# A transformer kernel with V and q products issued inside the feed-forward block, feed-forward weights split at the layer border, and the global norm's inverse on ScalarE

## The reference, cut to what matters

```
x = attn_layer(shift_tokens(x), Wqkv[i], q_scale[i], k_scale[i], Wo[i]) + x
x = ffn_layer(shift_tokens(x), ln_g[i], ln_b[i], W1[i], b1[i], W2[i], b2[i]) + x
```

## Time and profile before

| | |
|---|---|
| median of 3 runs | 3241.17 us (3239.01 to 3252.73) |
| profiled execution, its own time | 3247.59 us |
| its span, first to last instruction | 3245.8 us |
| busy share PE / DVE / ACT / POOL | 97% / 84% / 78% / 75% |
| mean granted TensorE clock | 0.988 of 2.4 GHz |

### The profile page before, as it was taken

The page is one execution under the profiler, slowest core; times in us unless marked ns, Lnnn a source line. Parts: engine busy times, 40 slices in busy tenths (PEclk is TensorE's granted clock), DMA queues, the critical chain, the costliest instruction groups (busy, mean ns, idle before and its releaser), DMA issues. The chain is left out here.

```text
span 3245.8 us, 151130 instructions
## 1 busy us (share of the span) xinstructions
PE 3132.2 (97%) x63141; PEld 2614.1 (81%) x63141; DVE 2712.8 (84%) x6367; ACT 2522.3 (78%) x5220; POOL 2442.1 (75%) x1536
## 2 busy tenths in 40 slices
PE   7869999999999999999999999999999999999996
PEld 6757888888888888888888888888888888888885
DVE  6559888888888888888888888888888888888883
ACT  3337888887888888888888888888888888788884
POOL 6458787787777777777777778777777777777773
PEclk9889999999999999999999999999999999999998
DMA  4551111132111122211122211122111122121111
GB/s 168 195 189 47 45 44 46 46 88 72 50 43 45 50 81 63 63 42 47 50 81 63 63 45 44 47 79 70 57 50 44 45 79 72 56 57 45 47 54 29
DMA packets 109237, 211.00 MB, mean 65 GB/s; under 512 B 19344, under 2 KB 40080, under 8 KB 104592
## 3 DMA queue, kind: packets, MB, share of 16 engines
q1 hardware_dynamic: 106544, 193.36, 20.2%
q10 hardware_dynamic: 2016, 7.98, 0.7%
HBM read 46.91 MB, written 28.53 MB: 23 GB/s over the span
## 5 line engine op out<-in xcount | busy, mean ns | idle before, releaser
L456 POOL TENSOR_TENSOR qks<-work 128x1024 f32<-128x1024 f32 x384 | 910.2, 2370 | 524.9 <-DVE work L1216 508.1
L843 PE MATMUL psum<-wparts,xhi 128*128 128x512 f32 x2304 | 788.6, 423 | 14.9 <-POOL xlo L442 8.0
L464 POOL TENSOR_TENSOR qkr<-qks,rnorm 128x1024 f32<-128x1024 f32 x384 | 731.5, 1905 | 0.4
L605 ACT ACTIVATE sq<-psum 128x512 f32<-128x512 f32 x768 | 455.3, 593 | 117.8 <-PE psum L843 90.0
L1214 DVE TENSOR_TENSOR work<-psum,rot 128x512 f32<-128x512 f32 x768 | 523.6, 682 | 6.1 <-ACT sq L605 3.7
L1187 DVE TENSOR_REDUCE ssq<-sq 128x8 f32<-128x512 f32 x768 | 475.9, 657 | 0.0
L843 PE MATMUL psum<-wparts,xlo 128*128 128x512 f32 x1152 | 454.5, 395 | 0.0
L927 PEld LDWEIGHTS psum<-probT,vsh 64*64 64x64 f32 x12288 | 326.2, 134 | 140.6 <-issue 140.2
L843 PEld LDWEIGHTS psum<-wparts,xhi 128*128 128x128 f32 x2304 | 380.1, 191 | 60.7 <-issue 7.7
L868 PE MATMUL psum<-kT,qTs 64*32 64x64 f32 x24576 | 421.5, 218 | 0.0
L868 PEld LDWEIGHTS psum<-kT,qTs 64*32 64x32 f32 x24576 | 359.6, 107 | 64.7 <-issue 64.0
(11 more groups left out here) (151 smaller groups left out, 6137.5 us busy)
## 6 DMA issues: line engine op xcount, KB each, us to landing
vsh<-vtok SPq DMA_DIRECT2D x384, 192.0 KB, 2.4
vsh<-vtok SPq DMA_DIRECT2D x384, 64.0 KB, 2.7
wsplit<-wstage SPq DMA_DIRECT2D x15, 1024.0 KB, 6.4
wparts<-wsplit SPq DMA_DIRECT2D x30, 512.0 KB, 4.1
xsh<-xs_in SPq DMA_DIRECT2D x192, 64.0 KB, 2.4
ff_x<-x_mid SPq DMA_DIRECT2D x96, 128.0 KB, 2.4
wraw<-Wqkv_dram SPq DMA_DIRECT2D x18, 512.0 KB, 4.1
wsplit<-wstage SPq DMA_DIRECT2D x5, 1066.0 KB, 8.1
```

The lines of the kernel that those rows point to most:

```text
L456: pool.tensor_tensor(qks[:, :, :], rcos, rsin, ALU.add).then_inc(s["add_ready"], 1)
L464: pool.tensor_tensor(qkr[:, n % 2, :, :], qks[:, :, :], rnorm[:, :].unsqueeze(2).to_broadcast([P, 2 * OCT, DH]), ALU.mult).then_inc(s["qkr ...
L605: act.activation(sq[:, w * OCT:(w + 1) * OCT, :], bank[w].rearrange("p (h n) -> p h n", n=DH), ACT.Square).then_inc(s[("sqq_ready", "sqk_r ...
L843: mm = pe.matmul(out, xparts[xp][:, ti, :], wparts[:, SECTION_AT[w, oc], wp_, :], start=(k == 0), stop=(k == 2))
```

## The change

Three edits.

1. `ffn_up` is cut in two. `ffn_gate_products` stays at place 1 but stands ahead of the V product; `ffn_values` moves to place 2, behind the next step's q product. PE's order is then: gates, V, (next step) q, values, transposed probabilities.
2. The feed-forward weights leave the split of the first stage. The raw weights of a layer (533 KB) are loaded to a new tile `wff_raw`: layer 0 by SyncE at the start, the others by ScalarE's queue at place 0. At place 14 of each layer's steps ACT copies the high part and at place 16 POOL subtracts the low part (six times each). PE waits for `wff_ready` before a block's gates. Eighteen pieces are left in the first stage, in portions of 2, 3, 3, 3, 3, 4 behind norms 2 to 7; four rotary tables instead of five stand ahead of the second norm.
3. `global_inverse` moves from POOL (add, power) to ACT: `Ln(var + eps)`, then `Exp(-0.5 x)`. In the tile loop it stands behind `exponential_global` at i = 0 (norm of the batch before) and i = 4 (norm of the next batch); the last one stands at the end of step 0 of the second stage, and POOL no longer does it ahead of `x_low`.

The diff, cut to its core:

```diff
-PIECES = len(SECTIONS) // 2 + 1
+PIECES = len(SECTIONS) // 2
...
+        wff_raw = sb("wff_raw", [P, FFW])
...
+            sp.dma_start(wff_raw[:, :], Wff[0]).then_inc(s["wff_in"], 16)
...
-            def global_inverse(n):
-                pool.wait_ge(s["gmv_ready"], n + 1)
-                pool.tensor_tensor(vare[:, :], mv[:, :, 1], eps_row[:, :], ALU.add).then_inc(s["gve_step"], 1)
-                pool.wait_ge(s["gve_step"], n + 1)
-                pool.tensor_tensor(rstd[:, :], vare[:, :], minus_half[:, :], ALU.pow).then_inc(s["grstd_ready"], 1)
...
-            global_inverse(0)
             pool.wait_ge(s["gain_in"], 16 * 2)
             pool.wait_ge(s["gvs_ready"], 2)
-            for layer in range(DEPTH - 1):
+            for layer in range(4):
                 rotary_gains(layer)
-            global_inverse(1)
             pool.wait_ge(s["gxn_ready"], 2)
-            rotary_gains(DEPTH - 1)
+            for layer in range(4, DEPTH):
+                rotary_gains(layer)
             done = 0
-            for n, pieces in ((1, 4), (2, 4), (3, 4), (4, 4), (5, 4), (6, 4)):
+            for n, pieces in ((1, 2), (2, 3), (3, 3), (4, 3), (5, 3), (6, 4)):
                 if n > 1:
-                    global_inverse(n)
                     pool.wait_ge(s["gxn_ready"], n + 1)
...
-            global_inverse(2 * B - 1)
-
...
+            def ffn_weights_low(layer):
+                if layer is None:
+                    return
+                pool.wait_ge(s["wff_hi"], layer + 1)
+                pool.tensor_tensor(wff[:, 1, :], wff_raw[:, :], wff[:, 0, :].bitcast(F32), ALU.subtract).then_inc(s["wff_ready"], 1)
...
             for step in range(STEPS + 3 * UNROLL):
+                ffn_weights_low(entered_at(step, 16))
                 gated_low(block_at(step, 5))
...
+            def global_inverse(n):
+                act.wait_ge(s["gmv_ready"], n + 1)
+                act.activation(vare[:, :], mv[:, :, 1], ACT.Ln, bias=eps_row[:, 0:1]).then_inc(s["gve_step"], 1)
+                act.wait_ge(s["gve_step"], n + 1)
+                act.activation(rstd[:, :], vare[:, :], ACT.Exp, scale=-0.5).then_inc(s["grstd_ready"], 1)
+
+            global_inverse(0)
...
+                    if i == 0 and b:
+                        global_inverse(NORM_AT[b - 1, 1])
+                    if i == 4 and b + 1 < B:
+                        global_inverse(NORM_AT[b + 1, 0])
...
-                act.wait_ge(s["f_y"], layer * BLOCKS)
-                act.dma_start(wff[:, :, :].bitcast(F32).rearrange("p h n -> p (h n)"), wsplit[layer - 1, PIECES - 1]).then_inc(s["wff_in"], 16)
+                act.wait_ge(s["wff_ready"], layer)
+                act.dma_start(wff_raw[:, :], Wff[layer]).then_inc(s["wff_in"], 16)
+
+            def ffn_weights_high(layer):
+                if layer is None:
+                    return
+                act.wait_ge(s["wff_in"], 16 * layer + 16)
+                need(act, "f_y", layer * BLOCKS)
+                act.activation(wff[:, 0, :], wff_raw[:, :], ACT.Copy).then_inc(s["wff_hi"], 1)
...
-                ffn_renewed(renewed_at(step, 14))
+                ffn_renewed(renewed_at(step, 0))
+                ffn_weights_high(entered_at(step, 14))
...
+                if step == 0:
+                    global_inverse(2 * B - 1)
...
-            def ffn_up(b, step):
+            def ffn_gate_products(b, step):
                 if b is None:
                     return
                 layer = b // BLOCKS
-                need(pe, "wff_in", layer * 16)
+                pe.wait_ge(s["wff_ready"], layer + 1)
...
+            def ffn_values(b):
+                if b is None:
+                    return
                 for ch in range(CH):
                     w = CW[ch]
                     pe.wait_ge(s["f_gel"], b * CH + ch + 1)
...
                 projection(step, 0)
+                ffn_values(block_at(step, 2))
...
                 ffn_down(block_at(step, 3), step)
+                ffn_gate_products(block_at(step, 1), step)
                 value_projection(step - 3)
-                ffn_up(block_at(step, 1), step)
```

More of the change, by code:

```diff
@@ L68, in renewed_at, with entered_at @@
     return layer if (step - place) % UNITS == 0 and 0 < layer < DEPTH else None
+def entered_at(step, place):
+    layer = (step - place) // UNITS
+    return layer if (step - place) % UNITS == 0 and 0 <= layer < DEPTH else None
 def last_block_at(step, place):
@@ L237, in raw_fetched @@
                 layer, k = j // PIECES, j % PIECES
[L238 to L241, removed]
+                sp.dma_start(wraw[:, j % 2, :, :].rearrange("p s n -> p (s n)"), Wqkv[layer][:, k * 1024:(k + 1) * 1024]).then_inc(wraw_in[j % 2], 16)
             def split_stored(j):
                 layer, k = j // PIECES, j % PIECES
-                width = 2 * FFW if k == PIECES - 1 else 4 * 512
-                sp.dma_start(wsplit[layer - 1, k][:, 0:width], wstage[:, j % 2, 0:width].bitcast(F32)).then_inc(w_stored[j % 2], 16)
+                sp.dma_start(wsplit[layer - 1, 2 * k:2 * k + 2].rearrange("s p n -> p s n"),
+                             wstage[:, j % 2, :, :, :].bitcast(F32).rearrange("p s h n -> p s (h n)")).then_inc(w_stored[j % 2], 16)
             raw_fetched(0)
@@ L269, in section_renewed @@
                 sp.wait_ge(s[("projq_ready", "projk_ready", "vp_ready")[w]], layer * UNITS - 1 + oc)
-                sp.dma_start(wparts[:, k, :, :].bitcast(F32).rearrange("p h n -> p (h n)"), wsplit[layer - 1, k // 2][:, k % 2 * 1024:k % 2 * 1024 + 1024]).then_inc(wparts_in[k], 16)
+                sp.dma_start(wparts[:, k, :, :].bitcast(F32).rearrange("p h n -> p (h n)"), wsplit[layer - 1, k]).then_inc(wparts_in[k], 16)
             def rotation_renewed(layer, half):
@@ L364, in _ @@
             pool.memset(ssq[:, :, 1], 1e-24)
-            pool.memset(eps_row[:, :], LNEPS)
+            pool.memset(eps_row[:, :], LNEPS).then_inc(s["ones_ready"], 1)
             pool.memset(mask[:, :, :, :], 0.0).then_inc(s["mask_ready"], 1)
@@ L403, in weights_split @@
                     pool.wait_ge(w_stored[slot], 16 * ((j - PIECES) // 2))
[L404 to L412, removed]
+                parts = wstage[:, slot, :, :, :] if layer else wparts[:, 2 * k:2 * k + 2, :, :]
+                pool.tensor_copy(parts[:, :, 0, :], wraw[:, slot, :, :]).then_inc(s["w_hi"], 1)
                 pool.wait_ge(s["w_hi"], j + 1)
-                pool.tensor_tensor(lo, raw, hi.bitcast(F32), ALU.subtract).then_inc(s["w_lo"], 1)
-            global_inverse(0)
+                pool.tensor_tensor(parts[:, :, 1, :], wraw[:, slot, :, :], parts[:, :, 0, :].bitcast(F32), ALU.subtract).then_inc(s["w_lo"], 1)
             pool.wait_ge(s["gain_in"], 16 * 2)
             pool.wait_ge(s["gvs_ready"], 2)
-            for layer in range(DEPTH - 1):
+            for layer in range(4):
                 rotary_gains(layer)
-            global_inverse(1)
             pool.wait_ge(s["gxn_ready"], 2)
-            rotary_gains(DEPTH - 1)
+            for layer in range(4, DEPTH):
+                rotary_gains(layer)
             done = 0
-            for n, pieces in ((1, 4), (2, 4), (3, 4), (4, 4), (5, 4), (6, 4)):
+            for n, pieces in ((1, 2), (2, 3), (3, 3), (4, 3), (5, 3), (6, 4)):
                 if n > 1:
-                    global_inverse(n)
                     pool.wait_ge(s["gxn_ready"], n + 1)
@@ L515, in _ @@
             act.activation(silu_t[:, 0, :], c_col[:, :], ACT.Exp, scale=-1.0).then_inc(s["silu_step"], 1)
+            act.wait_ge(s["ones_ready"], 1)
+            def global_inverse(n):
[4 more added lines that the diff above has]
+            global_inverse(0)
             act.wait_ge(s["modp_ready"], 1)
@@ L704, in ffn_renewed @@
                     return
-                if layer == 1:
-                    for half in range(2):
-                        act.wait_ge(w_stored[half], 16 * ((DEPTH * PIECES - PIECES + half) // 2))
-                act.wait_ge(s["f_y"], layer * BLOCKS)
-                act.dma_start(wff[:, :, :].bitcast(F32).rearrange("p h n -> p (h n)"), wsplit[layer - 1, PIECES - 1]).then_inc(s["wff_in"], 16)
+                act.wait_ge(s["wff_ready"], layer)
[6 more added lines that the diff above has]
+                act.activation(wff[:, 0, :], wff_raw[:, :], ACT.Copy).then_inc(s["wff_hi"], 1)
             act.wait_ge(s["const_in"], 16 * 2)
```

11 lines of the change are left out of this document (4 added, 7 removed).

## The result

The changed kernel takes 3197.24 us (median of 4 runs, 3194.67 to 3199.86); the kernel before took 3244.29 us beside it (4 runs, 3239.01 to 3252.73). The ratio is 0.9845, 95% interval [0.9833, 0.9857]: faster by 47 us in the medians, where 52 were forecast. The forecast time of 3189 us is 8 us short: 5 us of that are gain that did not come, 3 us are the kernel before, whose median was 3241.17 in the forecast and 3244.29 beside the changed kernel.

What follows compares the result with a forecast made beforehand. PE, 97% busy, was taken to bound the steady layers, and the engine-to-engine chain the first stage. First stage 28 us plus layers 24 us, together 52, from the median 3241.2 gave 3189 us; range 3172 to 3215.

Steps and rivals of the forecast that it cites:

- Part 1: Layers: gates ahead of V and values behind q close PE's wait for gelu, 47 blocks x 0.58 = 27 us.
- the 5.8 to 5.9: PE in a block: sign of being right, distance in us from k transposes to transposed probabilities.
- sign of being wrong on PE: L989 waiting for POOL's ff_lo well over 0.2 us, or L901 newly waiting for DVE's gel or POOL's probn.
- Rival (a): Layers: gates wait for POOL's low part or aoT, no longer covered by V; part 1 void, 3216 us; chance 0.11.
- Part 2: First stage: inverse on ACT removes DVE's waits of 9.19 and 8.76 us, 19.5 us with clock; stage border 2.3 us.
- Rival (b): First stage keeps half its waits, from ACT's queue behind an exponential or POOL's portions; 3203 us; chance 0.09.
- clock term: First stage: with full clock behind the removed waits, norm to next L1106 takes 13.7 instead of 14.7 us.
- contention term: First stage: shorter POOL portions free DVE's products with the scale (L1120) from POOL's subtracts, 5.5 us (bounds 0 and 6.4).
- Part 3: Weights: shorter first-stage portions gain 5.5 us; the split at six layer borders costs 3 us (bounds 0 and 21).
- Rival (c): Layer borders: the splits delay PE by the bound of 21 us instead of 3; 3207 us; chance 0.07.
- (d): Layers: values held behind V and q make DVE the bound, a slower kernel, about 3260 us; chance 0.03.
- (e): More gain than forecast: gates not late (8 us more), PE's clock stays up in the first stage; 3177 us; chance 0.10.

Runs made afterwards that it cites:

- the run with the old order: Changed kernel with PE's old order (V, gates, values) put back: 3220.59 us, ratio 0.992 to the kernel before.
- run with five tables: Changed kernel with five rotary tables instead of four ahead of the second norm: 3194.19 us, ratio 0.9832 to the kernel before.
- run with the low part later: Changed kernel with PE's wait for POOL's low part moved to the first gate's third product: 3200.21 us, ratio 0.985 to the kernel before.
- changed kernel again: The changed kernel measured a second time, unaltered, as baseline for later runs: 3195.88 us, ratio 0.984 to the kernel before.
- the run with the moved portions: Changed kernel with raw weights loaded at place 8, five rotary tables, portions of 2, 3, 3, 2, 3, 5: 3192.08 us.

## Why the prediction was right, and where its steps were not

The accounting of the two profiled executions: first gate at 344.89 and 315.14 us (29.8 us gained; forecast 28 to the end of the first stage), from there to the first gate of block 47 of the 48, 46 distances, 2838.57 and 2817.20 us (21.4 gained; forecast 24), tail 62.3 and 61.7 us. So the first stage gave 2 us more than forecast and the layers 2.6 less: the sum is nearer than its parts.

**Part 1 held in size and in mechanism.** The distance from the k transposes to the transposed probabilities fell from a median of 6.86 to 6.35 us, 0.51 where I had 0.59, and the distance of blocks from 61.57 to 61.00, 0.57 where I had 0.58. Counted from the end of the k transposes the first of these is 5.94 us, just outside the 5.8 to 5.9 that were named as the sign. The gates start 0.17 us late, as forecast (0.58 less 0.41); the passage of the semaphore, which I had put at 0.05 us without a row, is 0.10 us from the end of POOL's low part to the first gate, in all 48 blocks. The runs with PE's order alone (27 us) and with the order undone (23 us) give it twice. Neither sign of being wrong on PE, a new wait for DVE's `gel` or one for the low part well over 0.2 us, came. Rival (a) was a true neighbour: the two waits are there, in the order named, and taking away the first alone gave nothing because the second gate kept its start of 1.42 us.

**Part 2 had a right sum for a partly wrong reason, and that was luck.** The step that failed is "the waits of 9.19 and 8.76 us go" as the inverse's own doing. They stood for POOL's four-piece portions, and both edits remove them: the inverse alone gives 12.7 us, the weights alone 18, both together some 26 (the run with the old order against the kernel before). Undone in the changed kernel, the inverse is worth 8.5 us. I had credited it with 19.5, and with 2.3 more at the border of the stages. The change held both edits, so the waits went all the same and the sum stood; with the inverse alone it would have missed. Rival (b) as I wrote it did not come: DVE waits for ACT's `rstd` only once, 0.78 us at the last norm.

**The first stage by stretches.** The starts of the norms and of the first products behind them (L1106 or L1122) cut the stage into stretches. The first norm is that of the next batch (50.32 us in the kernel before), the second that of the batch before (87.06). In us, summed over the batches:

| stretch | before | after | gained | forecast |
|---|---|---|---|---|
| second norm to the next first norm, two times | 45.41 | 27.38 | 18.0 | 18.0, the waits |
| first norm to the first products, three times | 42.66 | 39.87 | 2.8 | 1.5, the clock |
| first products to the second norm, three times | 66.13 | 60.18 | 6.0 | 5.5, contention |
| start to the first of these norms | | | 0.3 | 0.6, batch 0 and first norm |
| last second norm to the first gate | | | 2.7 | 2.3, border of the stages |

**The clock term was under-sized.** Windows of the kernel before, then of the changed one, each from a norm to the next L1106 or L1122 (same columns as above):

```profile
50.32:64.03 13.71, 11.76 (x77) 10.36 (x76) 5.71 (x18) 5.00 (x8) 10.83 (x5) 0.88 0.39 154
109.98:124.71 14.73, 11.36 (x54) 9.74 (x55) 5.71 (x18) 5.00 (x8) 8.57 (x6) 0.63 0.82 294
```

```profile
50.02:62.10 12.08, 10.45 (x78) 9.08 (x79) 5.72 (x18) 5.40 (x9) 9.86 (x3) 1.00 0.22 90
97.46:109.54 12.08, 10.82 (x80) 9.08 (x79) 5.72 (x19) 5.40 (x9) 6.79 (x4) 1.00 0.88 312
```

I took batch 0 as the clean case; its granted clock was itself 0.88. In the two traces in which DVE waited 0.78 us ahead of this norm the stretch takes 13.7 us at 0.88; in all others the wait is 0.39 us or less, and it takes 12.07 or 12.08 us at 1.00. So batches 0 and 1 take 1.6 us less than I had assumed. Batch 2 does not: 15.71 us at a mean clock of 0.89, because of the slow norm.

**The contention term had the right size and missed one victim.** The products with the scale went from 3.57, 3.73 and 3.05 us for two to 3.31, 1.82 and 1.28, 3.9 us less in their own time; the stretches in which they stand are 6.0 us shorter, where I had 5.5. What lies between is at least in part the clock: with both products free this stretch takes 18.44 us at a granted clock of 1.00 and 19.63 at 0.91 (run with five tables, batches 1 and 0). What I had not priced is that a wait taken away moves what stood behind it: the norm of batch 2 fell onto POOL's delayed third piece. The norm lost 2.0 us itself, but its stretch takes 15.71 us instead of the free 12.08, 3.6 us more. Over the traces in which this norm meets the third piece's subtract that price runs from 1.8 us (run with the low part later, 13.83 us, clock 1.00) to 5.0 us (changed kernel again, 17.04 us, clock 0.80). Where the clock stayed at 1.00, three traces, the stretch is longer by the norm's own delay alone. It ate what the clock term had gained beyond its forecast.

**Part 3 at the layer borders cost more, and elsewhere.** 46 distances of 0.57 us are 26.2; 21.4 were gained, so the borders cost 4.8 us where I had 3. POOL's subtract, which I gave most of it, shows only as 0.9 us in 5 waits of PE on L891. The traces put the cost on the load at place 0: with the load at place 8 the borders are as cheap as in the kernel before (5.0 and 4.5 us over the median distances, against 6.2 before and 11.2 in the changed kernel). I had named that meeting of loads and left it within the 3 us. Rival (c) fell: 4.8 us, not 21. So did (d): DVE waits longer for the values (86.5 us against 73.9 in the layers), and PE's list of waits does not name DVE. Of (e), the clock of the first stage did rise, from 0.91 to 0.98, but the gates stayed late.

## What to carry to other kernels

A stall behind a long portion of background work is cured by cutting the portion as well as by moving the waiting operation to another engine, and two such cures overlap: price them together, not each against the old profile. When a wait goes, look up what the released instruction will now run beside, and price not only its own delay but the stretch behind it, where PE's clock may fall. A new load near others is priced by what lands late beside it, not by the engine work that comes with it. When a wait is removed without gain, look for the second wait directly behind it, and before an instruction is moved ahead in an in-order queue, price its wait in all steps in which it stands, not only in the one that wants it.

## What the runs showed of the hardware

A norm of one SBUF tensor, two columns and no second tensor (L1076, 128x128) takes 340 ns on DVE alone and took 2334 ns beside a 2.37 us subtract of POOL, ending 0.08 us behind it. A copy of POOL does the same: in the run with the inverse alone one norm took 1089 ns beside a 1.12 us CAST. In the prediction I had applied contention only to instructions with two SBUF tensors. The Trainium skill (SBUF — State Buffer, "Who interferes with whom") lists `tensor_scalar` among the operations that can enter a mode with both ports and then exclude GpSimd's; the traces agree in the blocking, in this kernel and in the run with the inverse alone (7.26 us for eight), though the mode itself no trace shows. In the run with the moved portions no subtract lies beside a norm, but for the last 0.19 us of one, and all 56 take 335 to 350 ns:

```profile
L1076 DVE TENSOR_SCALAR sq<-xtok,mv,rstd x56: 335/341/350, 8.0 to 171.5; 128x128 f32<-128x128 f32 x56
```
